# A macaron block (half FFN, attention, half FFN): key and query stacks transposed in three pieces, another order in attention batch 0, and the last FFN chunk by thirds

## The reference

```
x = x + 0.5 * ffn(layernorm(x))              # FFN 1
x = x + attn(layernorm(x))                   # attention
x = x + 0.5 * ffn(layernorm(x))              # FFN 2

ffn(y):  down( silu(gate(y)) * up(y) )       # 128 -> 384 -> 128, weights int / 127
attn(y): h = rmsnorm(y) * norm_w
         q, k, v = h@Wq, h@Wk, h@Wv          # 4 heads of 32; 2 k/v heads, each used by 2 heads
         q, k = l2norm(q), l2norm(k)
         a = softmax(causal(q @ k.T * exp(log_temperature)))
         return y + gate * ((a @ v) @ Wo)
```

## Time and profile before

| | |
|---|---|
| median of 3 runs | 429.08 us (427.14 to 429.15) |
| profiled execution, its own time | 429.13 us |
| its span from first to last instruction | 427.3 us |
| granted TensorE clock, mean | 0.996 |
| TensorE busy | 394.0 us, 92% |
| ScalarE busy | 371.0 us, 87% |
| VectorE busy | 348.8 us, 82% |
| GpSimdE busy | 288.5 us, 68% |

### The profile page before, as it was taken

One profiled execution on the slowest core, in us unless ns is written; L12 is line 12 of the kernel. 1 busy time (PEld: TensorE's weight loads), 2 busy tenths in 40 slices (PEclk: granted clock), 3 DMA queues, 4 the chain that ended last, 5 costly groups with the idle time before them and its releaser, 6 DMA issues.

```text
span 427.3 us, 13356 instructions
## 1 busy us (share of the span) xinstructions
PE 394.0 (92%) x5403; PEld 221.6 (52%) x5403; DVE 348.8 (82%) x903; ACT 371.0 (87%) x497; POOL 288.5 (68%) x365
## 2 busy tenths in 40 slices
PE   0689999898999799999999999999999999999995
PEld 0346666674454445535545546446454336676655
DVE  5889999689799978988988988957769938888565
ACT  4799999776898689899898998999988989999961
POOL 5679999986624956767768658662223558999951
PEclk9999999999999999999999999999999999999999
DMA  6487523513714417418347047046123115556452
GB/s 172 102 195 156 69 49 51 100 27 74 126 28 100 75 20 95 88 30 109 66 65 120 17 77 125 3 92 110 38 42 75 27 36 80 109 122 108 117 123 81
DMA packets 119298, 35.25 MB, mean 82 GB/s; under 512 B 101697, under 2 KB 119233, under 8 KB 119233
## 3 DMA queue, kind: packets, MB, share of 16 engines
q1 hardware_dynamic: 117952, 34.02, 43.3%
q10 hardware_dynamic: 1280, 0.33, 0.3%
HBM read 4.98 MB, written 4.19 MB: 21 GB/s over the span
## 4 chain that ended last, share of the span: by engine, by line
PE 59%; DVE 9%; ACT 9%; DMA 7%; POOL 7%; issue 5%; SPq 1%; ACTq 0%; DVEq 0%
PE ps L754 11%; PE ps L519 11%; PE ps L784 11%; PE ps L791 10%; PE ps L583 4%; PE ps L572 4%; DMA QKT<-ST 4%; PE ps L818 4%; ACT XN L471 3%; PE ps L608 3%; ACT PT L898 2%; PE ps L761 2%; DVE H L340 2%; POOL HL L446 2%; ACT SG L489 2%
## 5 line engine op out<-in xcount | busy, mean ns | idle before, releaser
L898 ACT ACTIVATE PT<-ps,k_exp 128x1024 f32<-128x1024 f32 x144 | 153.6, 1117 | 14.4 <-PE ps L761 7.9
L519 PE MATMUL ps<-XT,WT 128*128 128x512 f16 x384 | 94.0, 383 | 5.8 <-DVE H L340 1.9
L754 PE MATMUL ps<-QKT 128*32 128x512 f16 (+1 forms) x1280 | 86.7, 361 | 5.6 <-DMA QKT<-ST 4.5
L791 PE MATMUL ps<-PT,ones 128*32 128x512 f32 (+3 forms) x768 | 76.7, 488 | 0.0
L784 PE MATMUL ps<-PT,V 128*32 128x512 f32 (+3 forms) x768 | 76.3, 487 | 0.0
L446 POOL TENSOR_TENSOR HL<-H,HH 128x1024 f16<-128x1024 f32 x31 | 66.5, 2145 | 8.4 <-ACT HH L495 5.4
L340 DVE SCALAR_TENSOR_TENSOR H<-SG,k_isilu,ps 128x1536 f32<-128x1536 f32 x31 | 56.1, 1809 | 11.2 <-ACT SG L489 5.8
L519 PEld LDWEIGHTS ps<-XT,WT 128*128 128x128 f16 x384 | 34.4, 98 | 50.3 <-issue 10.1
L471 ACT ACTIVATE XN<-X,NB,RS 128x128 f32<-128x128 f32 x128 | 52.5, 483 | 2.4 <-POOL NB L418 2.4
L754 PEld LDWEIGHTS ps<-QKT 128*32 128x32 f16 x1280 | 31.9, 97 | 41.3 <-issue 22.6
L489 ACT ACTIVATE SG<-ps,k_silu 128x1536 f32<-128x1536 f32 x32 | 48.8, 1525 | 4.4 <-DVE H L340 4.3
(11 more groups left out here) (146 smaller groups left out, 671.2 us busy)
## 6 DMA issues: line engine op xcount, KB each, us to landing
result<-X SPq DMA_DIRECT2D x15, 256.0 KB, 2.5
X<-in_L_attn_x SPq DMA_DIRECT2D x7, 512.0 KB, 4.6
X<-in_L_attn_x SPq DMA_DIRECT2D x2, 256.0 KB, 4.7
XT<-w_int SPq DMA_TRANSPOSE x32, 3.1
QKT<-ST SPq DMA_TRANSPOSE x20, 5.5
AXT<-AS SPq DMA_TRANSPOSE x16, 2.8
w_int<-in_L_ffn_w_gate SPq DMA_DIRECT2D x1, 192.0 KB, 3.9
w_int<-in_L_ffn_w_up SPq DMA_DIRECT2D x1, 192.0 KB, 4.4
```

The costliest lines, as they stand in the source:

```text
L519: i = e.matmul(out[:, j, :], WT[:, wp, w * NJ + j, :], XT[k % 2][:, xp, :], start=a == 0, stop=a == len(passes) - 1)
L754: i_ = e.matmul(dst[r, :].rearrange("p (s a n) -> p s a n", a=2, n=P), QKT[k % 2][:, i // TPC, NH + hp, key0 + r.start:key0 + r.stop], q.r ...
L791: i_ = e.matmul(sums_of(h, 1, n), ones32[:, :], weights_of(g, h, o, n), start=i == 0, stop=i >= TPC * qc, skip_group_check=True)
L898: e.activation(dst, SCORES[(SLOT0[g] + i) % 2][:, :, :], ACT.Exp, scale=k_exp[:, 0:1]).then_inc(a_exp, 1)
```

## The change

Three things change.

1. **Pieces.** Without the row maxima (the path that this input takes) every stack is transposed in three DMAs of two blocks. For an even m these are the keys, the queries of the first head pair, and those of the second. For an odd m they are the two query pairs and then the keys. The scores wait for the piece that they use.
2. **Batch 0's order.** GpSimdE casts x of m = 2 and 3. VectorE normalises m = 5 behind QN of m = 3 and copies the high parts of m = 3 right after that, ahead of the statistics. ScalarE casts the stack of m = 3 one group earlier, and x of m = 5 behind the exps of the next batch's first group. GpSimdE's and SyncE's lists follow: the x transpose of m = 5 stands between the query pieces and the key piece of m = 3.
3. **End of FFN 2.** The down products of chunk 13 come before the up products of chunk 15. Chunk 15's up products are made in the order of thirds 1, 2, 0, H is made by thirds, ScalarE casts two thirds one by one, and GpSimdE and VectorE make one third of the low part each. Down products of chunk 15 start with the split thirds.

```diff
         def ffn_dve(...):
             def hidden(k, c):
+                if ph and k == NC - 1:
+                    for n, j in enumerate(LAST_ORDER):
+                        e.wait_ge(s_up_last, n + 1)
+                        e.scalar_tensor_tensor(H_LAST[:, j, :], SG[:, j, :], k_isilu[:, 0:1], U[:, j, :],
+                                               ALU.mult, ALU.mult).then_inc(s_h_last, 1)
+                    return
...
                     residual_of(c - 2, DN)
-                    e.wait_ge(s_hh, c + NC * ph + 1)
-                    e.tensor_tensor(hidden_parts(ph, k)[2][:, :], hidden_16(ph, k), hidden_parts(ph, k)[1][:, :], ALU.subtract)\
-                        .then_inc(s_hl_last, 1)
+                    e.wait_ge(s_hh_last, 2)
+                    last_split_of(e, 1).then_inc(s_hl_last, 1)
...
         def ffn_pe(...):
             def up(k, c):
                 if ph and k == NC - 1:
                     down_of(k - 2, c - 2)
+                    e.wait_ge(s_h, g)
+                    products(k, 1, U, sums_copied, LAST_ORDER, s_up_last)
+                    return
...
         def att_pe(...):
             def scores(k, b, g, hp):
+                elif g == 0:
                     if hp == 0:
-                        e.wait_ge(d_k0, 16)
-                        e.wait_ge(d_q0, 16)
+                        e.wait_ge(d_k0, b * 16 + 16)
+                        e.wait_ge(d_q0, b * 16 + 16)
                     else:
-                        e.wait_ge(d_t[0], 16)
+                        e.wait_ge(d_t[0], b * 16 + 16)
+                elif g == G0:
+                    e.wait_ge(d_q2 if hp else d_q1, b * 16 + 16)
+                elif g == NG - 3 and hp == 0:
+                    e.wait_ge(d_t[1], b * 16 + 16)
...
         def att_act(...):
-                        if k == 0 and g in (0, 1):
-                            x_hi(2 + g, g)
-                        if g == (9 if k == 0 else 8):
+                        if g == 8:
                             stack_hi(m0 + 1, 1)
                     if k + 2 < B and g == 7:
                         x_hi(m0 + 2, 0)
+                    if k + 2 < B and g == (9 if k == 0 else 7):
                         x_hi(m0 + 3, 1)
...
         def turn(e, shift):
-                stack(m, 0, NQK, d_t[m % 2])
+                elif m % 2:
+                    stack(m, 0, 2, d_q1)
+                    stack(m, 2, NH, d_q2)
+                    if m == 3:
+                        turn_x(e, 5)
+                    stack(m, NH, NQK, d_t[1])
+                else:
+                    stack(m, NH, NQK, d_k0)
+                    stack(m, 0, 2, d_q0)
+                    stack(m, 2, NH, d_t[0])
```

More of the change, by code:

```diff
@@ L493, in h_hi @@
                     return
+                if ph and k == NC - 1:
+                    for n in range(NJ - 1):
+                        cols = slice(n * CH, (n + 1) * CH)
+                        e.wait_ge(s_h_last, n + 1)
+                        e.activation(HH_LAST[:, cols], hidden_16(ph, k)[:, cols], ACT.Copy).then_inc(s_hh_last, 1)
+                    return
                 e.wait_ge(s_h, c + NC * ph + 1)
@@ L512, in ffn_pe, with products @@
         def ffn_pe(e, ph, low, only=None, after={}, banks_read=None):
-            def products(k, w, out, bank_free=lambda j: None):
+            def products(k, w, out, bank_free=lambda j: None, order=range(NJ), done=None):
                 passes = [(0, 0), (0, 1)] + [(1, 0)] * low
-                for j in range(NJ):
+                for j in order:
                     bank_free(j)
@@ L520, in products @@
                                      start=a == 0, stop=a == len(passes) - 1)
+                    if done is not None:
+                        i.then_inc(done, 1)
                 return i
@@ L537, in up @@
                 g = c + NC * ph
-                if k >= 1 or ph:
+                if (k >= 1 or ph) and not (ph and k == NC - 1):
                     e.wait_ge(s_h, g)
@@ L552, in down, with last_down, split_products @@
                     down_of(k, c)
+            def last_down(dn, full, split):
+                def split_products(hp, wp, j, first=False):
+                    for t, j_ in split:
+                        if j_ == j:
+                            o = j * CH + t * P - CUT
+                            i = e.matmul(dn[:, t, :], (HH_LAST, HL_LAST)[hp][:, o:o + P], WT[:, wp, 2 * NJ + j, :],
+                                         start=first and t == 0, stop=hp == 1, skip_group_check=True)
+                    return i
+                for j in LAST_ORDER[:-1]:
+                    e.wait_ge(s_hh_last, j)
+                    for wp in range(1 + low):
+                        split_products(0, wp, j, j == 1 and wp == 0)
+                e.wait_ge(s_h_last, NJ)
+                for t, j in full:
+                    e.matmul(dn[:, t, :], H_LAST[:, j, t * P:(t + 1) * P], WD[:, j, :], start=False, stop=False,
+                             skip_group_check=True)
+                e.wait_ge(s_hl_pool, 1)
+                split_products(1, 0, 1)
+                e.wait_ge(s_hl_last, 1)
+                split_products(1, 0, 2).then_inc(s_dn, 1)
             def down_of(k, c):
                 g = c + NC * ph
-                e.wait_ge(s_h, g + 1)
+                if not (ph and k == NC - 1):
+                    e.wait_ge(s_h, g + 1)
                 if ph and k == 0:
@@ L1039, in att_pool @@
             stack_lo(1, 1)
-            x_lo(2, 0)
-            x_lo(3, 1)
+            for half in range(2):
+                first_x_hi(2 + half, half)
+                x_lo(2 + half, half)
             def step(k, b):
@@ L1064, in step @@
                     x_lo(m0 + 2, 0)
+                if later and k >= 1:
                     x_lo(m0 + 3, 1)
@@ L1254, in step @@
                     normalise(m0 + 2, m0 + 2, q)
-                if later:
+                if later and k >= 1:
                     normalise(m0 + 3, m0 + 3, q + 1)
@@ L1347, in turn @@
                     qk(1)
-                for half in range(2):
-                    if k + 1 < B:
-                        turn_x(e, 2 * k + 2 + half)
-                if k:
+                if k + 1 < B:
+                    turn_x(e, 2 * k + 2)
+                if k + 1 < B and (k != 1 or shift):
+                    turn_x(e, 2 * k + 3)
+                if k >= 1:
                     qk(2 * k + 1)
```

52 lines of the change are left out of this document (28 added, 24 removed).

## The result

The changed kernel took 424.61 us (median of 5 runs, 424.22 to 424.94), the kernel before 429.08 (median of 5, 427.14 to 429.99). The ratio is 0.9908, 95% interval 0.9889 to 0.9927: 4.5 us less, where 4.7 were forecast. The profiled execution after has a span of 423.0 us and took 424.82.

The account below looks back on a forecast made before the run. TensorE, busy 92% of the span, was taken as the bound, with gains only where it stands still. From 429.1, -3.1 - 1.0 - 0.6 = -4.7 us gave 424.4 us, range 422.0 to 427.0.

Parts of the forecast that it names:

- Batch 1, -3.1: Attention's batch 1: the wait for the stack of m = 3 goes, group 4's scores start at 147.1, 3.1 us less.
- The price of the fallen clock: TensorE in batch 1: the slow clock level after a long wait would cost at most some 1.7 us.
- The landings: Query pieces of m = 3: issued about 135.5, landing about 138.7 and 140.0, 3 to 4 us ahead of use.
- The cover of 1.2 us for x's m = 5: Batch 1, ahead of group 3: this x transpose lands at 141.4, TensorE asks for it at about 142.6.
- Batches 2 and 3, -1.0: Attention: earlier query pieces remove 1.0 us of the 1.07 above two steady batches (29.66 us each, no wait).
- The end, -0.6: End of FFN 2: chunk 13's down products fill TensorE's 0.58 us wait for H of chunk 14; 0.6 us less.
- The first: Batch 0 into 1: VectorE's reciprocal and OH come early too, batch 1 gains 5.1 us: 422.4 us; chance 0.18.
- The second rival: Batch 1: TensorE's clock falls again after waiting for exps, costing some 1.7 us: 426.1 us; chance 0.12.
- The third: Every batch: the stack's last piece lands 16.5 us after the first issue, TensorE waits: 442 us; chance 0.04.
- the fourth: Batch 1: AXT of m = 5 or OH slips 2 us more, only the wait moves: 426.9 us; chance 0.10.
- The signs: Profile checks: QKT waits under 0.3 us, clock 1.00, OH about 145, batch 1 31 to 32 us, batches 4-6 29.66.

## Why the prediction was right

**Batch 1, -3.1: measured -3.0, by the way that was forecast.** OH was left at 144.95 and started at 144.76; group 3's exps were put at 146.0 and started at 145.78; group 4 at 147.1, measured 146.94; batch 2 at 164.4, measured 164.52. The clock stayed at 1.00. The price of the fallen clock, put at 1.7 us at most, is 1.50 by the two profiled executions, those of before and of the kernel with the new end alone, and 1.4 by the two kinds of runs. So about a third of the gain against the median of before is the clock, which often fell behind the late stack; against the runs of before without that, after gains 2.9 us. The text did not say that the fall comes in some executions only. That the change was measured against a median at the level of the runs with the fall (429.08), as the forecast took it, was luck. A profile and three runs could have hinted at it (427.14 against 429.08 and 429.15).

**The landings were too optimistic, at no cost.** The stack of m = 3 was issued at 136.01 (135.5 forecast), but its query pieces landed at 140.98 and 142.84 and not at 138.7 and 140.0. The step gave each piece the shortest landing of the earlier trace rows; after, a piece of this tile takes 3.9 us by the median and 5.5 at most. Against the 143.8 at which TensorE wants them, 2.8 us were to spare for the first piece and 1.0 for the second, and not 3 to 4. The last of three pieces was put at 5.8 us behind the issue of the first; from m = 4 on it takes 5.8 to 8.4. The fixed cost of about 2.0 us that the prediction names from the Trainium skill ("DMA: Bandwidth & Descriptors", section "Anatomy of one DMA — SWDGE (gpsimd) path") is stated there for DMAs that GpSimdE issues, and these are SyncE's; the sum did not use it.

**The cover of 1.2 us for x's m = 5 was not there.** Its issue began at 138.71 (138.2 forecast), took 2.88 us behind the two pieces where the x transpose ahead of it took 1.23, and landed at 143.59 instead of 141.4. TensorE waited 0.78 us for it. The text said that such a wait would be taken from the one for exps, and that held: removing it (group 3 at 143.25) gained nothing.

**Batches 2 and 3, -1.0: measured -1.07, with a cause that is half right.** Pieces are not the only way to that gain, and part of its size is luck. With whole stacks these two batches took 1.07 us more than two steady ones in before, 0.27 in the kernel with the new end alone, 0.50 in the one with whole stacks from m = 4 on, and nothing in the one with the new order alone. The stack of m = 5 was issued 2.4 us behind the start of batch 2 in both of the first two; it took 8.6 us to land in before (169.91 to 178.49) and 6.5 with the new end alone (168.87 to 175.35), early enough for its use. So one whole stack of this size is late in one execution and not in another. What makes it land late is not shown; what it meets in the queue is a guess. In the three traces in which a whole stack came late, pieces would have had 0.3 to 1.1 us to gain. The 1.4 us of the medians without them is more than that, and half of what its trace shows stands in FFN 2.

**The end, -0.6: measured -0.53, of which the forecast's own path gave 0.40.** Chunk 13's down products filled the wait of 0.58, and the low thirds were in time. The 0.6 was worked out for TensorE's last row, and that moved 0.40: a wait of 0.24 us for a residual, which the step had not listed, took the rest. The other 0.13 stands behind TensorE's last row.

**A term that was missing: +0.30 ahead of the end of FFN 2.** TensorE waited 0.36 us at 387.55 for the transposed input of one chunk. The same wait, 0.3 to 0.4 us, is in nine of the twelve experiments, with the old end and with the new one, and not in before or in the three others. What sets it stays open; the transposes' place among other DMAs is my guess.

**The rivals.** The first (OH early too, 422.4) had put a steady batch behind an early OH. The experiments refute that: OH 1.1 us earlier gave nothing, then AXT, QN and the stack of m = 4 took over in turn, and the lowest median without leaving work out was 424.17, not told apart from after. Nor did the new order free VectorE: what GpSimdE's low parts cost it only moved. Before and then after, the four normalisations behind the statistics, and the second of the two copies of the high parts, each of them beside a low part of GpSimdE in one trace and not in the other:

```profile
136.60 2.31 DVE L720 TENSOR_SCALAR X<-X,A,B 128x128 f32<-128x128 f32 x4
...
139.03 0.22 DVE L1171 COPY ST<-ST 128x256 f16<-128x256 f16 x1
```

```profile
134.26 1.18 DVE L1227 COPY ST<-ST 128x256 f16<-128x256 f16 x1
...
137.94 1.08 DVE L770 TENSOR_SCALAR X<-X,A,B 128x128 f32<-128x128 f32 x4
```

The second rival did not happen in any of the runs of after, whose mean clock was 1.00. The third had no trace of it: the last piece landed at most 8.4 us behind the issue of the first from m = 4 on, and not 16.5. Of the fourth one half came: AXT slipped by 2.2 us against its forecast landing, and it cost nothing. Its sum is off too: gains of 1.2 and 1.3 us lead to 426.6, not 426.9.

**The signs.** Three of them were narrowly missed: batch 1 took 32.03 us (31 to 32), one wait for QKT of 0.4 us is left (0.3), in batch 0, and TensorE's last row moved 0.40 us (0.6). The others came: OH at 144.76, a granted clock of 1.00 all through attention, batches 2 to 6 at 29.66.

## What to carry to other kernels

A long wait of TensorE can hide a tie. Before pricing its removal, read in the lists of the engines that feed it what would release the same instruction next, and what would come after that: here four conditions followed each other so closely that OH 1 us earlier gave nothing. Two edits that each remove the same wait do not add. And where a long wait can let the clock fall, look at the granted clock of every run: two kinds of runs, 1.4 us apart, hid a gain of 0.5 us.

## What was unexpected of the hardware

The same 2.80 us wait of TensorE was followed by the lower clock level in one execution and not in another (3.48 and 2.38 us from group 3 to group 4), so one trace without the fall does not prove that it is gone. And the issue of one small transpose (x of one half) on SyncE took from 1.23 to 2.88 us, the longest right behind two pieces of another tile.
